# Both halves of the k projection in the slots ahead of the turned maxima: a decoder layer on one Trainium2 core

## The reference: what is computed

```python
x = x + self_attention(layernorm(x), W, b)        # 16 heads of 16, causal softmax
x = x + cross_attention(layernorm(x), ctx, Wq, Wkv, Wc)   # 120 context rows per sequence
x = x + ffn(layernorm(x), W_router, W1, b1, Wo, bo, gamma, beta)  # the chosen one of 4 experts
```

```python
qkv = einsum('btc,oc->bto', x, W) + b
att = softmax(where(causal, einsum('bhtd,bhsd->bhts', q, k) / sqrt(D), -inf))
y = einsum('bhts,bhsd->bhtd', att, v)
```

## Time and profile before

| | |
|---|---|
| three runs | 3292.09, 3295.55, 3298.89 us |
| the profiled execution's own time | 3280.96 us |
| its span, first to last instruction | 3279.1 us |
| mean granted TensorE clock | 0.981 of full speed |
| TensorE busy | 3058.4 us (93%) |
| DVE busy | 2565.8 us (78%) |
| ACT busy | 1753.8 us (53%) |
| POOL busy | 1272.7 us (39%) |

### The profile page before, as it was taken

One profiled execution on the slowest core, in us unless ns is written; L12 is line 12 of the kernel. 1 busy time (PEld: TensorE's weight loads), 2 busy tenths in 40 slices (PEclk: granted clock), 3 DMA queues, 4 the chain that ended last, 5 costly groups with the idle time before them and its releaser, 6 DMA issues.

```text
span 3279.1 us, 78416 instructions
## 1 busy us (share of the span) xinstructions
PE 3058.4 (93%) x26632; PEld 2417.7 (74%) x26632; DVE 2565.8 (78%) x6882; ACT 1753.8 (53%) x3260; POOL 1272.7 (39%) x1773
## 2 busy tenths in 40 slices
PE   3899999999999999999999999999849999999998
PEld 2677777777777777777777777777539999999997
DVE  2687888788788888878888887888638888888886
ACT  1465555556555655555565565556424545454543
POOL 3233333333333333333333343333214545455554
PEclk8999999999999999999999999999869999999999
DMA  5665556556556655655565565566233333434341
GB/s 100 88 110 111 98 109 115 104 99 113 112 96 111 112 103 103 112 106 98 111 112 104 102 115 107 99 107 107 56 110 136 128 138 128 142 123 146 122 149 47
DMA packets 321569, 359.70 MB, mean 110 GB/s; under 512 B 62040, under 2 KB 289631, under 8 KB 321248
## 3 DMA queue, kind: packets, MB, share of 16 engines
q1 hardware_dynamic: 308384, 321.96, 47.8%
q0 software_dynamic: 12864, 33.64, 3.1%
HBM read 140.93 MB, written 46.21 MB: 57 GB/s over the span
## 4 chain that ended last, share of the span: by engine, by line
PE 85%; DVE 8%; issue 4%; DMA 1%; SPq 1%; POOL 0%; ACT 0%; DVEq 0%; POOLq 0%
PE psum L624 15%; PE psum L986 12%; PE psum L970 12%; PE psum L619 8%; PE psum L723 4%; PE psum L811 4%; PE psum L701 3%; PE psum L710 3%; PE psum L677 3%; PE psum L674 3%; PE psum L789 3%; PE psum L668 3%; DVE negmax L1207 2%; PE psum L803 2%; PE psum L827 2%
## 5 line engine op out<-in xcount | busy, mean ns | idle before, releaser
L1039 ACT ACTIVATE PA<-psum 128x512 f32<-128x512 f32 x512 | 305.9, 598 | 354.6 <-PE psum L710 350.5
L1207 DVE TENSOR_REDUCE negmax<-psum 128x2 f32<-128x512 f32 x512 | 344.2, 683 | 106.8 <-PE psum L677 99.7
L1144 ACT ACTIVATE hT_high<-psum,b_sb 128x512 fp32r<-128x512 f32 x280 | 193.2, 690 | 415.2 <-PE psum L970 393.2
L1045 ACT ACTIVATE PC<-psum 120x512 f32<-120x512 f32 x512 | 303.8, 596 | 206.4 <-PE psum L803 205.6
L1204 DVE TENSOR_REDUCE negmax<-psum 128x4 f32<-128x512 f32 x256 | 177.0, 691 | 250.0 <-PE psum L677 243.8
L1212 DVE TENSOR_REDUCE cnegmax<-psum 128x4 f32<-128x480 f32 x512 | 324.5, 644 | 7.6 <-PE psum L789 7.4
L986 PE MATMUL psum<-wo_high,hT_low 128*128 128x256 f32 x1120 | 319.8, 286 | 0.6 <-DVE hT_low L1488 0.6
L986 PE MATMUL psum<-wo_low,hT_high 128*128 128x256 f32 x1120 | 316.9, 283 | 0.0
L986 PE MATMUL psum<-wo_high,hT_high 128*128 128x256 f32 x1120 | 316.9, 283 | 0.0
L1488 DVE TENSOR_TENSOR hT_low<-hT,hT_high 128x512 fp32r<-128x512 f32 x280 | 267.0, 972 | 52.4 <-ACT hT L1145 52.4
L624 PE MATMUL psum<-zT,wqk_sb 128*128 128x256 f32 x1024 | 266.3, 383 | 2.9 <-DVE q_rest L1230 2.2
(11 more groups left out here) (211 smaller groups left out, 8255.3 us busy)
## 6 DMA issues: line engine op xcount, KB each, us to landing
QP<-q_parts SPq DMA_DIRECT2D x384, 128.0 KB
KP<-k_parts SPq DMA_DIRECT2D x384, 128.0 KB, 4.2
QC<-cq_parts SPq DMA_DIRECT2D x384, 128.0 KB, 3.9
w_high<-w_high_dram SPq DMA_DIRECT2D x35, 1024.0 KB, 5.1
w_low<-w_low_dram SPq DMA_DIRECT2D x35, 1024.0 KB, 7.0
fx<-rows_dram SPq DMA_DIRECT2D x35, 514.0 KB
x_in<-in_x SPq DMA_DIRECT2D x64, 256.0 KB, 4.7
x_res<-in_x SPq DMA_DIRECT2D x64, 256.0 KB, 5.1
```

The costliest lines, as they stand in the source:

```text
L1039: act.activation(dst, psum[:, ST_BANKS[n % 2], :], ACT.Exp, scale=D ** -0.5).then_inc(exp_done.sem, 1)
L1045: act.activation(PC[0:M, 2 * n:2 * n + 2, :].rearrange("p h n -> p (h n)"), psum[0:M, ST_BANKS[n % 2], :], ACT.Exp, scale=D ** -0.5).then_ ...
L1144: act.activation(hT_high[:, m, :], psum[:, m % 4, :], ACT.Gelu, bias=b1_sb[:, q, m:m + 1])
L1207: dve.tensor_reduce(negmax[:, 1, h:h + 2], bank.rearrange("p (h k) -> p h k", h=2), AX_X, ALU.max).then_inc(max_done.sem, 1)
```

## The change

TensorE's order alone changes. `project_k(i + 1, 0)` goes from slot 19 to slot 18, `project_k(., 1)` from slot 0 of its own iteration to slot 19 of the one ahead, and in slot 0 `cross_values(i - 4, par, 0, ...)` goes ahead of the turning of the maxima. The semaphores, and the orders of DVE, ACT, POOL and SyncE, are as before.

```diff
@@ -854,13 +854,11 @@
-                    if n == 0 and runs(i, 0):
-                        project_k(i, 1)
+                    if n == 0 and runs(i, 4):
+                        cross_values(i - 4, par, 0, latest((y_scaled, i - 2, 1), (kmask_made, i - 3, 1), (cyT_copied, i - 5, 1)))
                     if n == 0 and runs(i, 1):
                         pe.wait_ge(*latest((place_step, i - 5, 5), (czT_copied, i - 3, 1)))
                         turn_max(i - 1, mx_split, mxT_made, mx2, 6)
-                    if n == 0 and runs(i, 4):
-                        cross_values(i - 4, par, 0, latest((y_scaled, i - 2, 1), (kmask_made, i - 3, 1), (cyT_copied, i - 5, 1)))
                     if n == 1 and runs(i, 4):
                         cross_values(i - 4, par, 1, None)
@@ -919,8 +917,10 @@
                     if n == 17 and runs(i, 4):
                         logits(i)
+                    if n == 18 and runs(i, -1):
+                        project_k(i + 1, 0)
                     if n == 19 and runs(i, -1):
-                        project_k(i + 1, 0)
+                        project_k(i + 1, 1)
                     if n == 19 and runs(i, 1):
                         turn_y(i - 1, 1, yT_copied, yt_made, yT, 5)
```

## The result

| | before | after |
|---|---|---|
| median (lowest to highest), ten runs each | 3290.59 us (3287.32 to 3298.89) | 3305.70 us (3298.97 to 3312.91) |
| the profiled execution's own time, span | 3280.96, 3279.1 us | 3304.39, 3302.5 us |
| mean granted TensorE clock | 0.981 | 0.979 |

The ratio of after to before is 1.0038, with a 95% interval from 1.0028 to 1.0048. The change makes the kernel slower by 0.4%: 15.1 us by the medians, 12.5 us by the ratio. The profiled executions lie 23.4 us apart, because that of before was an unusually short one.

What follows compares the result with a forecast made beforehand. TensorE, busy 93% of the span, bounds the kernel; its waits at slot 8 and the maxima's turn decide. Slot 8 0.22 us later in 60 iterations gives 13 us, on a 3295.55 us median: 3308.5 us, range 3299 to 3316.

Steps and rivals of the forecast that it cites:

- Slot 18: First half of k in slot 18: its wait for q_rest costs nothing; DVE's last self maximum stays covered by 0.18 us.
- The rival of 3322 us: Cover ahead of DVE's last self maximum fails; find_rows, k_rest and all behind come 0.4 to 0.5 us late; chance 0.1.
- Second half to slot 19, cross_values ahead of the turn: Slots 19 and 0: rank, so find_rows, 0.20 us late; cross_values in front makes the turn 0.22 us later.
- The gain is waited away in slot 3: Turning of cyT in slot 3: TensorE, about 0.3 us ahead, loses that in a new wait for k_rest.
- The slot 8 wait: TensorE's wait at L668 for k's packs: 1.3 to 1.4 us after the change, from 1.14 us.
- The landing follows the turn: k's packs at slot 8 land the whole 0.22 us later, with the start of the burst; bounds 0 and 0.33.
- the pair's 1.49 to 1.09 us: Two iterations before: high packs took 1.09 us more to issue, scores in slot 8 started 1.49 us later.
- The lower bound of 0: Slot 8 landing not delayed if the DMA engines had room for the burst's later start: 0 us.
- The Trainium skill's rule for one DMA: k's last packs: an estimated 2.3 us for 128 KB, landing follows its own issue, sum 0 instead of 13 us.
- The faster rival: SyncE's high packs, 0.22 us later, stretch less often: 9 us faster, 3287, or all gone 20 us; chance 0.15.
- if the high packs' issue stopped stretching: SyncE's issue of k's high packs: a sign in the profile after that the forecast would be wrong.
- The sum: Slot 8's release 0.22 us later an iteration, 60 iterations, 13 us; forecast 3308.5 us.

Runs made afterwards that it cites:

- e1: Changed kernel with the turning of the maxima put back ahead of cross_values(0) in slot 0; 3309.20 us, 1.0054 of before.
- e2: Changed kernel with turn_y and rank put ahead of the second half of k in slot 19; 3317.45 us, 1.0081 of before.
- e3: Changed kernel with turn_y and rank ahead of k's second half, and the turn ahead of cross_values(0); 3287.63 us, 0.9988 of before.
- e4: Kernel before with the turning of the maxima moved from slot 0 to slot 1, behind its two score groups; 3364.52 us, 1.0224 of before.
- e12: Kernel before with k_rest made in slot 1, its rounding in slot 2, POOL's low part ahead of its root; 3293.22 us, 1.0005 of before.
- e9: e4 with five useless matmuls of 512 columns put into the wait ahead of slot 8; 3336.18 us, 1.0130 of before.
- e10: e2 with five useless matmuls of 512 columns put into the wait ahead of slot 8; 3305.63 us, 1.0035 of before.
- e5: Kernel before with rank's counts in bank 4 instead of 6, so the turn no longer waits for find_rows; 3283.06 us, 0.9973 of before.

## Why the prediction held, step by step

*Slot 18.* Free, as costed. The cover of DVE's last self maximum held as well: the mask matmul that fills its bank started 0.45 us ahead of it (994.40 to 994.85), 0.18 us of it slack behind its end, the 0.18 us of the prediction. The rival of 3322 us falls with that.

*Second half to slot 19, cross_values ahead of the turn.* +0.20 and +0.22 us were predicted as two limits, +0.20 was measured, and e1, e2 and e3 show that both are there. This is the step on which the sum rests.

*The gain is waited away in slot 3.* Right in kind, short in place. From cross_values to the turning of cyT in slot 3 it was 0.57 us before (1027.83 and 1028.40) and is 0.77 now (1001.23 and 1002.00), since k_rest ends at 1001.95: 0.2 us go there, of the 0.3 predicted. The list of TensorE's matmul waits has only 0.6 us of it, because the weight load took the wait. Its own waits (PEld is the weight load) over 165 to 2290 us, before and then after, have 0.2 us an iteration more:

```profile
PEld psum L619 <- DVE k_rest L1230: 24.7, 60, 0.4
```

```profile
PEld psum L619 <- DVE k_rest L1230: 36.5, 59, 0.8
```

The 24.7 us are a wait that the prediction's "Nothing else repeats" passed over, since it read the matmuls alone. The rest, and what more there was to gain, went to **slot 5, which the prediction did not look at**. DVE's cz took 1.67 us there instead of 0.73, and V stands behind it. DVE's cz in all iterations of the steady stretch (count, busy, mean ns, idle before), before and then after:

```profile
L1189 DVE TENSOR_SCALAR cz<-x,cmv,crstd 128x256 f32<-128x256 f32 x120 | 44.4, 412 | 1.1 <-POOL crstd L1572 1.1
```

```profile
L1189 DVE TENSOR_SCALAR cz<-x,cmv,crstd 128x256 f32<-128x256 f32 x118 | 92.6, 826 | 1.1 <-POOL crstd L1572 1.1
```

The same instruction takes twice as long on average. POOL's row beside it, and the second of the two cz by itself:

```profile
1002.79 1.16 POOL L1629 TENSOR_TENSOR k_parts<-k_rest,k_parts 128x512 bf16<-128x512 f32 x1 [0.84 <-ACT k_parts L1003]
```

```profile
1002.75 1.34 DVE L1189 TENSOR_SCALAR cz<-x,cmv,crstd 128x256 f32<-128x256 f32 x1
```

cz ends at 1004.09, POOL's low part of k at 1003.95. Before, the low part began at 1029.23, when the cz (1028.63 to 1029.36) were nearly through. The change brought ACT's rounding 0.3 us nearer to the copy of the maxima (it ended 5.07 us behind it instead of 5.37, since the cross scores of slot 3, whose exponential stands ahead of it on ACT, come sooner behind the turn) and POOL's low part with it, right onto the second cz. 53 of 59 pairs of cz are over 1.2 us after, 1 of 60 before. The Trainium skill ("SBUF — State Buffer", section "Who interferes with whom") has a rule for it: a tensor_scalar in a two-port mode and a GpSimd instruction exclude each other, and the second to come waits until the first has ended. The trace agrees that one of them waits for the whole of the other: the 1.34 us end 0.14 us behind POOL's. It doesn't show in which mode cz runs. Which of the two waits is decided by very little. In after, cz waited in 52 iterations in which its record starts 0.04 to 0.05 us ahead of POOL's; in 49 of e2 it starts 0.06 to 0.09 us ahead, and there POOL's instruction took longer, 1.36 us instead of 1.16 in most. So the start in the record is not yet the moment that counts.

*The slot 8 wait.* Predicted 1.3 to 1.4 us, measured 1.08. The V wait of 16.1 us in 59 iterations is 0.27 of it, taken three slots earlier. The sum is 1.35 us. It cost nothing in time by itself, since the slot 8 wait behind it took it up. Perhaps it even paid: split in two places, the waits at slot 8 are shorter, and there were four half-clock stretches against e2's eleven.

*The landing follows the turn.* I took 0.22 us, one for one, with 0 and 0.33 as bounds, the upper one from the pair's 1.49 to 1.09 us. For a turn that is 0.20 us later, the copy to slot 8 grew by 0.10 us more, in the medians of after, e1 and e2 alike (12.09, 12.12 and 12.10, against 11.99 before and in e3). That looks like 0.30 us an iteration, near the upper bound, but in after it is two things. In the 39 iterations without a stretched issue (a send of the maxima or a pack of k that takes 1 us or more to issue) the copy to slot 8 has a median of 11.68 us, against 11.66 before: one for one, as predicted. The extra is in the 20 iterations with one, with a mean of 12.77 us against 12.50 in 22 before. e1 is like after in this (11.63 without a stretch); in e2 the iterations without one are later too (11.97), and no run says why. In e4, 0.76 us bring 0.21 to 0.36 more by mean and median, 1.3 to 1.5 for one. The lower bound of 0, by which the landing follows its own issue, is excluded by e4 and e12. The Trainium skill's rule for one DMA ("DMA: Bandwidth & Descriptors", section "Anatomy of one DMA"), against which the prediction set the row, stands on that side, and the trace does not agree: the last packs took 4.4 us and, issued sooner, 5.3 us.

*The faster rival.* It said that stretched issues of the high packs cost the slot 8 wait some 0.56 us on average, and that moving them 0.22 us might avoid them. The first part of its picture moved: iterations with a pack of k that took over 0.4 us too long to issue went from 22 to 8. But 13 sends of the maxima just ahead of them were stretched instead, where there was none before. One of those after, 2.75 us instead of 1.18:

```profile
455.27 2.75 SPq L492 DMA_DIRECT2D QP<-mxT  x2
```

22 iterations have a stretch before and 20 after, and behind the copy the landing is later in them than before (12.77 and 12.50 us). The rival had a real effect and the wrong hope for it. The prediction also named it as a sign of being wrong ("if the high packs' issue stopped stretching"): that sign came in part, without the gain that would have gone with it.

*The sum.* Predicted 0.22 us by 60, 13 us, on a base of 3295.5: 3308.5. The measured difference is 12.5 us by the ratio and 15.1 by the medians. The turn alone is 12 us (0.20 by 60), one for one, so **the term on which the forecast rests came out in kind and in size**. What it lacked is the longer landing behind stretched issues, 0.10 us by 60 or 6 us in the profiled execution; 12 and 6 are a little more than was measured, and what gave the rest back is not shown. The half clock, 6.6 us of after's profiled execution, was not in the forecast either. It belongs to the 23.4 us between the two profiled executions (12, 6 and 6.6), but not to the change: the mean clock of the other executions is 0.978 on both sides. The base was 5 us too high, from a median of three executions where ten give 3290.59, and the difference 2 us too low against the medians. That the forecast lies within 3 us of 3305.7 is owed in part to these two errors having opposite signs.

## What to carry to other kernels

Where an instruction waits, look for a second limit of about the same size before moving work: here what was put in front of the turn and what was put in front of its input each cost the same 0.20 us, and undoing either alone showed nothing. Look at when the first of a set of transfers starts: the order with k_high ahead of the copy of the maxima gained 1.2%, issuing the last ones sooner gained nothing. Look at where TensorE's idle time is gathered, not only at its sum: with the slack in one wait instead of two the clock fell more often. And take the clock of many executions before calling a difference between two profiled ones an effect of the change.

## What the runs showed of the hardware

- TensorE's granted clock fell from 2.4 to 1.2 GHz behind single waits at slot 8, with TensorE 82% busy in the 13 us ahead of the one shown. The four in after stood behind waits of 1.85, 1.87, 1.93 and 2.23 us; other waits of 1.92 to 2.24 us had none behind them. Each cost 1.66 us. Five matmuls in the wait removed 14 of 15 (e9) and 11 of 11 (e10).
- A DVE tensor_scalar of 128x256 float32 took 0.41 us alone and 1.34 us beside a POOL tensor_tensor of 128x512 that began 0.04 us behind it. In 49 iterations of e2 POOL's began 0.06 to 0.09 us behind, and it was POOL's that took longer, 1.36 us instead of 1.16 in most. With 0.28 us neither did (before).
- SyncE's stretched issues (1 us or more instead of 0.6) seem to stay with a moment rather than with an instruction: the work moved by 0.2 us, and 13 of 20 fell on the transfer ahead, where none had been. What makes them is not shown.
- A turn 0.76 us later delays the landing by 1.0 to 1.1 us; one 0.34 us earlier (e5) brings it forward by only 0.04 (means). That asymmetry was not expected, and its cause is open.
